# Perceiver cross-attention kernel: order of the low-part products in each tile, order of the first tile, and the place of two quarters of a weight split

## The reference

```python
x = x + xattn(layernorm(x), ctx, ctx)     # x: 1 x 256 x 512, ctx: 1 x 25088 x 512
x = x + attn(layernorm(x))                # 16 heads, causal, 256 tokens
x = x + ffn(layernorm(x))                 # 8 experts, one per token

def xattn(q, k, v):
    qp = q @ Wq.T + bq                    # 256 x 128
    kp = k @ Wk.T + bk                    # 25088 x 128
    vp = v @ Wv.T + bv
    z = sigmoid(qp @ kp.T / sqrt(128))    # 256 x 25088, no normalisation
    return z @ vp
```

## Time and profile before

| | |
|---|---|
| median of three timed runs | 622.24 us |
| the profiled execution, its own time | 623.9 us |
| its span, first to last instruction | 622.0 us |
| TensorE matmul busy | 597.9 us, 96% of the span |
| VectorE busy | 457.5 us, 74% |
| ScalarE busy | 378.6 us, 61% |
| mean granted clock of TensorE | 0.985 of full |
| DMA, mean over the span | 186 GB/s |

### The profile page before, as it was taken

The page is one execution under the profiler, slowest core; times in us unless marked ns, Lnnn a source line. Parts: engine busy times, 40 slices in busy tenths (PEclk is TensorE's granted clock), DMA queues, the critical chain, the costliest instruction groups (busy, mean ns, idle before and its releaser), DMA issues.

```text
span 622.0 us, 7576 instructions
## 1 busy us (share of the span) xinstructions
PE 597.9 (96%) x3010; PEld 488.9 (79%) x3010; DVE 457.5 (74%) x461; ACT 378.6 (61%) x435; POOL 8.9 (1%) x10
## 2 busy tenths in 40 slices
PE   7899999999999999999999999999999979997897
PEld 4688888888888888888888888888888837784796
DVE  4867778787787877778777787877878768876444
ACT  5676756667666676756667666676666626564221
POOL 1000000000000000000000000000000040000000
PEclk9899999999999999999999999999999988999799
DMA  8666855868557465564646556465562700000000
GB/s 344 246 221 260 320 222 221 327 251 322 207 220 264 168 262 189 218 235 175 266 170 237 213 192 254 170 253 196 210 243 96 271 1 2 0 1 2 0 1 35
DMA packets 17971, 116.36 MB, mean 187 GB/s; under 512 B 2256, under 2 KB 2704, under 8 KB 4624
## 3 DMA queue, kind: packets, MB, share of 16 engines
q1 hardware_dynamic: 17360, 115.29, 49.1%
q10 hardware_dynamic: 576, 0.59, 0.3%
HBM read 115.35 MB, written 0.52 MB: 186 GB/s over the span
## 4 chain that ended last, share of the span: by engine, by line
PE 89%; DVE 6%; ACT 2%; DMA 1%; issue 1%; SPq 0%; DVEq 0%
PE ps L373 43%; PE ps L331 21%; PE ps L348 11%; PE ps L656 4%; PE ps L681 2%; PE ps L608 2%; PE ps L472 1%; PE ps L559 1%; DMA rawt<-in_ctxt 1%; PE ps L489 1%; DVE wul L404 1%; PE ps L589 1%; PE ps L633 1%; ACT w L573 1%; ACT th L261 0%
## 5 line engine op out<-in xcount | busy, mean ns | idle before, releaser
L373 PE MATMUL ps<-nh,zl 128*128 128x512 f32 x392 | 159.6, 407 | 0.5 <-DVE zl L363 0.5
L373 PE MATMUL ps<-nh,zh 128*128 128x512 f32 x392 | 154.6, 395 | 1.8 <-ACT zh L362 1.8
L373 PE MATMUL ps<-nl,zh 128*128 128x512 f32 x392 | 153.2, 391 | 0.0
L317 DVE TENSOR_TENSOR nl<-rawn,nh 128x2048 fp32r<-128x2048 f32 x49 | 112.3, 2293 | 27.6 <-issue 27.3
L358 ACT ACTIVATE zf<-ps 128x512 f32<-128x512 f32 x98 | 58.6, 598 | 106.5 <-PE ps L348 100.5
L363 DVE TENSOR_TENSOR zl<-zf,zh 128x1024 fp32r<-128x1024 f32 x49 | 60.0, 1225 | 84.6 <-ACT zh L362 84.6
L254 DVE TENSOR_TENSOR tl<-rawt,th 128x2048 fp32r<-128x2048 f32 x47 | 107.3, 2284 | 0.0
L373 PEld LDWEIGHTS ps<-nh,zl 128*128 128x128 f32 x392 | 73.9, 188 | 28.7 <-DVE zl L363 13.8
L315 ACT ACTIVATE nh<-rawn 128x2048 fp32r<-128x2048 f32 x49 | 93.5, 1908 | 0.0
L252 ACT ACTIVATE th<-rawt 128x2048 fp32r<-128x2048 f32 x47 | 89.7, 1909 | 0.0
L373 PEld LDWEIGHTS ps<-nl,zh 128*128 128x128 f32 x392 | 73.9, 189 | 16.5
(11 more groups left out here) (163 smaller groups left out, 669.2 us busy)
## 6 DMA issues: line engine op xcount, KB each, us to landing
rawn<-in_ctxn SPq DMA_DIRECT2D x49, 1024.0 KB, 4.8
rawt<-in_ctxt SPq DMA_DIRECT2D x48, 1024.0 KB, 5.6
wd_s<-in_wd SPq DMA_DIRECT2D x2, 1024.0 KB, 8.3
wu_s<-in_wu SPq DMA_DIRECT2D x1, 2048.0 KB, 7.7
wg_s<-in_wg SPq DMA_DIRECT2D x1, 2048.0 KB, 7.5
rawt<-in_ctxt SPq DMA_DIRECT2D x2, 512.0 KB, 6.4
wv_s<-in_wvt SPq DMA_DIRECT2D x1, 1024.0 KB, 8.4
wq_s<-in_wq SPq DMA_DIRECT2D x1, 1024.0 KB, 7.9
```

The source lines that it names most:

```text
L317: Nl[b] = put("vector", lambda e: e.tensor_tensor(nl[b % 2][:], rawn[b % 2][:], nh[b % 2][:], ALU.subtract), [n_ld[b], Nh[b]] + [AV[k] for ...
L373: AV[b] = put("tensor", lambda e, z=z, n=n, i=i, j=j, r=r: e.matmul(bank(4 + r), z[:, j * T + r * P:j * T + r * P + P], n[:, j * D:(j + 1) ...
```

## The change

The three passes of `values` are put in another order: zh x nh, zl x nh, zh x nl. In the first row group (j = 0) the loops over r and pass are swapped, so that both halves r do zh x nh, then both zl x nh, then both zh x nl. `values` can also wait for halves of `nh` and `nl`, where a tile has them (tile 0).

In the first tile all three passes of keys(0) stand ahead of the query projection. keys(1) moves behind scores(0). `nh` and `nl` of tile 0 are made in halves by `first_n`, behind the weights of tile 0, and the sum into `zacc` stands behind them. `qpl` waits for `qph`. For the tiles after the first, `weight_sum` is called after keys(b+1), which issues only TensorE instructions.

At the end two of the four quarters of the split of `wu` stay where they were; the other two are made after `yta` and `ytv`.

```diff
-        for k in range(2):
-            half_h(0, k, T0[k])
+        half_h(0, 0, T0[0])
         half_l(0, 0, T0[0])
+        half_h(0, 1, T0[1])
...
+        def weight_sum(b):
             ZA[b] = put("vector", lambda e: e.tensor_tensor(zacc[:], zacc[:], zf[:], ALU.add),
...
+            passes = [(zh[b % 2], n_h), (zl[b % 2], n_h), (zh[b % 2], n_l)]
             for j in js:
+                turns = [(r, i) for i in range(3) for r in range(2)] if j == 0 else \
+                    [(r, i) for r in range(2) for i in range(3)]
+                for r, i in turns:
+                    z, n = passes[i]
+                    nH, nL = Nh.get((b, j // 2), Nh[b]), Nl.get((b, j // 2), Nl[b])
+                    wait = {0: [ZH[b], nH], 1: [ZL[b]], 2: [nL]}[i]
...
-        keys(0, (0, 1))
+        keys(0)
         for c in range(4):
...
-        m = put("scalar", lambda e: e.activation(qph[:], ...), [m, DBK], "qph")
+        half_h(1, 0, t_ld[1])
+        key_parts(0)
+        QPH = put("scalar", lambda e: e.activation(qph[:], ...), [QP_PE, DBK], "qph")
         QP = put("vector", lambda e: e.scalar_tensor_tensor(
-            out=qpl[:], in0=bank(6)[:, 0:T], scalar=bqk_s[:, 0:1], in1=qph[:], op0=ALU.add, op1=ALU.subtract), [m], "qpl")
-        keys(0, (2,))
-        half_h(1, 0, t_ld[1])
+            out=qpl[:], in0=bank(6)[:, 0:T], scalar=bqk_s[:, 0:1], in1=qph[:], op0=ALU.add, op1=ALU.subtract),
+            [QPH], "qpl")
         half_l(1, 0, t_ld[1])
-        key_parts(0)
         half_h(1, 1, t_ld[1])
         half_l(1, 1, t_ld[1])
-        split_n(0)
+
+        def first_n(k):
+            n = HALF[k]
+            Nh[0, k] = Nh[0] = put("scalar", lambda e: e.activation(nh[0][:, n], rawn[0][:, n], ACT.Copy), [n_ld[0]], "nh")
+            Nl[0, k] = Nl[0] = put("vector", lambda e: e.tensor_tensor(
+                nl[0][:, n], rawn[0][:, n], nh[0][:, n], ALU.subtract), [n_ld[0], Nh[0, k]], "nl")
+            n_rd[0] = [Nh[0], Nl[0]]
+            if k == 1:
+                load_n(2)
...
-        keys(1)
         for b in range(NB):
...
                 scores(b)
                 weights(b)
-                if b:
-                    keys(b + 1)
+                keys(b + 1)
+                if b == 0:
+                    first_n(0)
+                    first_n(1)
+                weight_sum(b)
                 key_parts(b + 1)
                 split_n(b + 1)
...
-        for WUP in parts_of(wu_s, wuh, wul, [DWU, KP[NB - 1]], "wu"):
-            pass
+        wu_parts = parts_of(wu_s, wuh, wul, [DWU, KP[NB - 1]], "wu")
+        next(wu_parts)
+        next(wu_parts)
         values(NB - 1, (0, 1, 2))
...
                 YT.append(put("vector", lambda e, s=src: e.tensor_copy(yT[:, :, P:T], s), [f], "ytv"))
+        for WUP in wu_parts:
+            pass
```

More of the change, by code:

```diff
@@ L368, in values @@
             n_h, n_l = nh[b % 2], nl[b % 2]
+            passes = [(zh[b % 2], n_h), (zl[b % 2], n_h), (zh[b % 2], n_l)]
             for j in js:
[L370 to L376, removed]
-        keys(0, (0, 1))
+                turns = [(r, i) for i in range(3) for r in range(2)] if j == 0 else \
[4 more added lines that the diff above has]
+                    wait = {0: [ZH[b], nH], 1: [ZL[b]], 2: [nL]}[i]
+                    AV[b] = put("tensor", lambda e, z=z, n=n, i=i, j=j, r=r: e.matmul(
+                        bank(4 + r), z[:, j * T + r * P:j * T + r * P + P], n[:, j * D:(j + 1) * D],
+                        start=(b == 0 and i == 0 and j == 0), stop=(b == NB - 1 and i == 2 and j == 3)),
+                        wait, "av" if (i, j, r) == (2, 3, 1) else None)
+        keys(0)
         for c in range(4):
@@ L382, in program @@
         QP_PE = m
-        m = put("scalar", lambda e: e.activation(qph[:], bank(6)[:, 0:T], ACT.Identity, bias=bqk_s[:, 0:1]), [m, DBK], "qph")
+        half_h(1, 0, t_ld[1])
+        key_parts(0)
+        QPH = put("scalar", lambda e: e.activation(qph[:], bank(6)[:, 0:T], ACT.Identity, bias=bqk_s[:, 0:1]),
+                  [QP_PE, DBK], "qph")
         QP = put("vector", lambda e: e.scalar_tensor_tensor(
-            out=qpl[:], in0=bank(6)[:, 0:T], scalar=bqk_s[:, 0:1], in1=qph[:], op0=ALU.add, op1=ALU.subtract), [m], "qpl")
-        keys(0, (2,))
-        half_h(1, 0, t_ld[1])
+            out=qpl[:], in0=bank(6)[:, 0:T], scalar=bqk_s[:, 0:1], in1=qph[:], op0=ALU.add, op1=ALU.subtract),
+            [QPH], "qpl")
         half_l(1, 0, t_ld[1])
-        key_parts(0)
         half_h(1, 1, t_ld[1])
         half_l(1, 1, t_ld[1])
-        split_n(0)
+        def first_n(k):
[6 more added lines that the diff above has]
+                load_n(2)
         late = [(wv_s[:], wvt), (kvd_s[:], kvd), (wq_s[:], wq), (qr_s[:], qrope), (kr_s[:], krope), (kup_s[:], kup),
@@ L431, in program @@
                 weights(b + 1)
+                weight_sum(b + 1)
                 values(b, (2, 3))
```

## The result

The changed kernel took 617.68 us as median of four runs (615.72 to 618.19), the kernel before 622.43 (four runs, 621.68 to 623.51). The ratio is 0.9917, with an interval of 0.9889 to 0.9944: faster by 0.8%. Repeated on another chip, it gave 617.90 (five runs) against 623.87 (25 runs), ratio 0.9925, 0.9899 to 0.9951. The prediction said 615.4, in a range from 611.5 to 618.9.

What follows compares the result with a forecast made beforehand. The prediction took TensorE's stream to bound the 49 tiles. Gains of 0 (pass order), 4.1 (first tile) and 2.7 us (end), 6.8 in all, came off the median 622.24 to give 615.4, range 611.5 to 618.9.

Steps and rivals of the forecast that it cites:

- Part 1: New pass order in every tile: 0, since zl is still first needed by the third matmul; bounds -5.3 to +4.9 us.
- The rival by which the low part comes later: Every tile: a position is gained and the 0.11 us stall goes, 5.3 us less, 610.1; chance 0.06.
- The rival of pauses: Every tile: waiting for nl and changing PSUM banks pause TensorE; 0.2 us a tile gives 625; chance 0.06.
- The size of the stall: Third and fourth values matmuls of each tile: waiting for zl loses 0.11 us, 5.3 us over 48 tiles.
- Part 2: First tile: -4.1 us, of it 2.4 from the order and 1.64 from the slow clock; bounds -1.9 and -4.8.
- `tl`(2) was not late: Sign in the first tile: tl(2) fits by 0.3 us; the prediction fails if VectorE is late for it.
- Part 3: End of the stream: -2.7 us, Wv matmuls 1.36 earlier and the slow clock gone; bounds -0.6 and -3.1.
- Both clock terms: Slow clock gone in tile 0's values, 1.64 us, and in the Wv matmuls at the end, 1.6 us.
- the clock falls stay: Rival: both slow stretches come again, or elsewhere where TensorE is the bound; 3.2 less gain, 618.6; chance 0.12.

Runs made afterwards that it cites:

- the order alone: Kernel before with only the new order of the passes in values, in every tile: 624.44 us, ratio 1.001 to the kernel before.
- The trials at the second and the fifth place: Changed kernel with zl first read by each tile's second matmul: 628.48 us; or, from tile 1 on, by the fifth: 609.23 us.
- `zl` fifth: Changed kernel with zh x nh, zh x nl, zl x nh for both halves in turn from tile 1 on: 609.23 us, ratio 0.977 to the kernel before.
- the split alone: Kernel before with only the split of wu made in two places: 621.41 us, ratio 0.9966 to the kernel before.
- first tile alone: Changed kernel with old passes from tile 1 on and all four wu quarters in the old place: 619.29 us, ratio 0.9939 to the kernel before.
- changed kernel again: The changed kernel rerun without any edit, for the spread of its executions: 617.00 to 619.06 us.
- the trials with extra matmuls: Changed kernel with ten extra matmuls in each of the two later layernorms: 614.13 us; the same with zl also read by the fifth matmul: 606.14 us.

## Why the prediction was right, and where it was off

**Part 1, the order in every tile: right at 0.** The tiles kept their length (457.26 and 457.82 us over 47 in the changed kernel, 457.67 before), the wait stayed at the third matmul, and the order alone gave a ratio of 1.001. (From scores to scores a tile takes 9.80 before; the forecast's 9.77 was added from the pieces of tile 1.) The trials at the second and the fifth place show the reason and not only the result: what counts is how many matmuls stand ahead of the first reader of `zl`, and the edit leaves two. The rival by which the low part comes later falls; it would have been worth more than I said. The rival of pauses falls too: with the order alone, 47 tiles take 0.15 us more than before, where this rival needed at least 6.8.

The rule of the Trainium skill on cycling through PSUM banks ("TensorE: Matmul & The Clock Gate", section "A second HAM failure mode: psum-queue depth-cycling") is not borne out by these runs. Its case is a bf16 kernel; here the operands are fp32r, of the same 512 columns, and changing banks alone neither makes TensorE idle nor lowers its clock. With a bank change after every matmul the distance stays 0.2267 us, and over 453 us of tiles the granted clock is 1.00 (view of windows, `zl` fifth):

```profile
27.00:480.00 453.00, 453.00 (x2266) 385.99 (x2265) 353.94 (x236) 309.72 (x286) 0.00 (x0) 1.00 0.62 233
```

**The size of the stall was too small.** I took 0.11 us a tile, from three starts. Taking it away gave 0.17 to 0.18. What was mis-sized is the undisturbed distance: I set it at 0.228, out of a piece that itself held the disturbance, where it is 0.2267; and I looked at one matmul behind the wait only. In the timeline of the changed kernel the ones that follow are still far apart:

```profile
481.28 0.73 PE L379 MATMUL ps<-nh,zl 128*128 128x512 f32 x2
481.61 1.90 ACT L315 ACTIVATE nh<-rawn 128x2048 fp32r<-128x2048 f32 x1
481.85 0.63 PE L379 MATMUL ps<-nl,zh 128*128 128x512 f32 x2
```

The two `zl` matmuls take 0.57 us start to start, 0.12 above 0.453, and the next two and several more stand at 0.23 or a little over. Why the rate comes back only slowly behind the wait was not tried.

**Part 2, the first tile: -4.1 forecast, -3.92 measured in the span.** The steps came out near to the number: scores(0) 15.92 for 15.8, `zl` 19.36 for 19.15, the first half of `nl` ready at 21.7 for 21.6, scores(1) 26.44 for 26.3. TensorE waited 1.18 us for `qpl`, as the steps had it, and `tl`(2) was not late. By the first tile alone it is 3.8 to 4.6. The shares of order and clock can be told apart from the second half of `th`(0) to scores(1): with the old order at a slow clock it takes 21.06 us (before) and 21.27 (the split alone), with the old order at full clock 19.73 (the order of the passes alone), with the new one 17.12, 17.09 and 17.12 (changed kernel, first tile alone, changed kernel again). So the order gives 2.6 us, forecast 2.4, and the clock 1.3 to 1.5, forecast 1.64.

**Part 3, the end: -2.7 forecast, -2.69 measured in the span**, and the quarters are hidden. But the shares were off: the order gives 1.00, not 1.36, since the Wv matmuls started 1.99 us behind `ya` and not 1.95, and in the old order, undisturbed, 3.09 and not 3.33; the clock gives 1.69, not 1.6.

Both clock terms have a flaw of reading. They set distances between starts (22 x 0.228 = 5.02, 16 x 0.43 = 6.9) against the length of a whole piece (6.66, 8.48). Like against like, with the undisturbed pieces measured later, it is 6.66 - 5.32 = 1.34 and 8.48 - 7.13 = 1.35. That is also why 1.36 and 1.6 are more than the 2.7 of the part.

**Where the 2.3 us to the median went.** From the profiled execution alone the forecast for its like was 617.1, and 615.72 came, 1.0 of it by luck behind the last layernorm. For the median it was 615.4, and 617.68 and 617.90 came. The mis-sized term is the clock: I took 3.2 us of the 6.8 from two slow stretches of one execution of 623.9 us, and subtracted all of it from a median of 622.24. The ten traces show how often these stretches came:

| where the clock fell | old order there | new order there |
|---|---|---|
| `values` of tile 0 | 2 of 3 (before, split alone; not: passes alone) | 0 of 7 |
| Wv matmuls | 2 of 3 (before, passes alone; not: first tile alone) | 0 of 7 |

So in the changed kernel both stretches are gone wherever a trace was taken, but the kernel before does not always have them. An execution of before that lacks one has less to gain. That accounts for part of the 2.3 us; how large a part is not shown, because on the first chip no clock is on record for the other executions of before. On the chip of the repeat 22 of its 25 executions had 0.986 or less, and there the median fell by 5.97, nearer to 6.8.

The other side is the changed kernel itself. Five of its nine executions had a mean clock of 0.988 or 0.989, below both traced ones (0.994 and 0.991), with spans of 615.4 to 617.2. Where their further slow stretch lies is open, since none of the five was traced. The two traces differ behind the last layernorm, and the trials with extra matmuls show what the later layernorms hold in all: 3.8 us by the medians, mean clock up to 0.997 and 1.000.

The rival "the clock falls stay", 618.6, was nearer to the median than my forecast, though its reason is not what the traces show: neither fall came back in its place. That one comes at another place in the five untraced executions is possible: in the trace with the split alone, where the fall at the Wv matmuls is gone, the clock from 511 to 520 is 0.62, before 0.81.

## What to carry to other kernels

When an operand comes late, count how many instructions stand ahead of its first reader; a new order that leaves the count leaves the stall, and two places more made 8.7 us here. Take the undisturbed rate from a stretch without any stall, and add up what is lost behind the stall as well. Compare distances with distances and lengths with lengths. A slow stretch of the clock seen in one trace is worth its size only times its share of executions; filling the idle time ahead of it was the surer gain.

## What was not expected of the hardware

Ten extra bf16 matmuls (2.11 us busy, nine of them in the trace) in an idle time of under 3 us (2.77 in the changed kernel), in each of two layernorms, go with a clock at its upper level through both, in both traces that have them. They made the kernel faster though they compute nothing: 3.8 us.

```profile
504.31 2.11 PE L235 MATMUL ps<-wz 128*128 128x512 bf16 x9
...
507.04 0.66 PE L229 MATMUL ps<-id_s,h_s 128*128 128x128 f32 x4 [0.62 <-DVE h_s L220]
```

The transposes behind them waited for `h_s`, not for them. Idle time does not always lower the clock: in the first tile of the old order, TensorE is idle for 1.77 us ahead of the first `values` matmul in all three traces, and the clock fell in two of them. A stall of 0.11 us on a weight load cost TensorE's stream 0.17 to 0.18 us.
